# A four-layer gated cross-attention and FFN kernel: last residuals, LayerNorm roots and expert-weight loads put elsewhere in the engines' orders

## What is computed

```python
for l in range(4):
    x = x + tanh(g_xattn[l]) * xattn[l](layernorm(x), ctx, mask[l])   # 16 heads of 8
    x = x + tanh(g_ffn[l])   * ffn[l](layernorm(x))
# ffn[0]: silu(q4(x) q4(Wg)) * (q4(x) q4(Wu)), quantised by blocks of 16 again, times q4(Wd); 352 hidden
# ffn[1]: layernorm(x + relu(x W1 + b1) W2 + b2) * gamma + beta; 512 hidden
# ffn[2]: fp8(x * s) fp8(W) / (s * sw) + bias, s from the largest |x| of all batches
# ffn[3]: 16 experts of 128, the best 4 of a token, and 2 shared ones: silu(x Gate) * (x Up) Down
```

## Time and profile before

| what | value |
|---|---|
| median of 3 runs | 836.82 us |
| lowest and highest of them | 831.85 and 840.69 us |
| the profiled execution, whole | 837.56 us |
| its span (first to last instruction) | 835.8 us |
| PE, DVE, ACT, POOL busy, share of the span | 77%, 68%, 38%, 28% |
| mean granted clock of PE, 1 is full speed | 0.833 |

### The profile page before, as it was taken

One profiled execution on the slowest core, in us unless ns is written; L12 is line 12 of the kernel. 1 busy time (PEld: TensorE's weight loads), 2 busy tenths in 40 slices (PEclk: granted clock), 3 DMA queues, 4 the chain that ended last, 5 costly groups with the idle time before them and its releaser, 6 DMA issues. The chain is left out here.

```text
span 835.8 us, 9972 instructions
## 1 busy us (share of the span) xinstructions
PE 644.8 (77%) x2926; PEld 401.8 (48%) x2926; DVE 564.6 (68%) x1521; ACT 321.0 (38%) x611; POOL 236.1 (28%) x438
## 2 busy tenths in 40 slices
PE   5778786466769999784888880358887898989997
PEld 3434333244655664453544430124334576767875
DVE  8674788988772563486736645873557798878655
ACT  3043362133224425363144340213545455545554
POOL 4301233111111223104250631001122444545463
PEclk9576796878869999896599995555998889999999
DMA  8864321002203332005135320121500133343341
GB/s 252 177 186 129 57 71 30 0 1 64 63 12 100 109 58 82 13 1 161 28 105 151 76 78 0 50 77 58 167 14 3 53 105 98 93 124 104 113 120 57
DMA packets 67989, 67.71 MB, mean 81 GB/s; under 512 B 25119, under 2 KB 48223, under 8 KB 67552
## 3 DMA queue, kind: packets, MB, share of 16 engines
q1 hardware_dynamic: 61326, 64.61, 27.9%
q10 hardware_dynamic: 6610, 2.47, 1.2%
HBM read 50.29 MB, written 17.60 MB: 81 GB/s over the span
## 5 line engine op out<-in xcount | busy, mean ns | idle before, releaser
L1167 DVE TENSOR_REDUCE mraw<-ps 128x4 f32<-128x308 f32 x256 | 115.7, 475 | 81.6 <-PE ps L1550 33.0
L734 ACT ACTIVATE PT<-ps 110x512 f32<-110x512 f32 x192 | 110.9, 596 | 142.6 <-PE ps L1590 69.1
L1550 PE MATMUL ps<-KG,QG 98*128 98x308 f32 x256 | 115.3, 491 | 50.4 <-DVE mraw L1167 36.3
L1550 PEld LDWEIGHTS ps<-KG,QG 98*128 98x128 f32 x256 | 61.3, 246 | 95.9 <-DVE mraw L1167 72.6
L644 POOL TENSOR_TENSOR sg<-sg,cb 128x512 f32<-128x512 f32 x64 | 83.3, 1304 | 78.2 <-ACT sg L892 75.1
L1590 PE MATMUL ps<-QG,KG 128*110 128x512 f32 x192 | 95.6, 519 | 6.6 <-ACT PT L734 5.1
L1406 DVE TENSOR_TENSOR ps<-ps,sg 128x512 f32<-128x512 f32 x72 | 50.2, 698 | 39.2 <-POOL sg L644 36.0
L1610 PE MATMUL ps<-PT,VN 128*18 128x512 f32 x512 | 73.3, 647 | 0.0
L508 POOL CAST mhl<-mraw 128x64 fp32r<-128x64 f32 x16 | 5.0, 314 | 223.1 <-DVE mraw L1167 210.4
L1590 PEld LDWEIGHTS ps<-QG,KG 128*110 128x110 f32 x192 | 36.1, 192 | 51.9 <-ACT PT L734 37.1
L892 ACT ACTIVATE sg<-ps 128x512 f32<-128x512 f32 x72 | 43.2, 599 | 46.1 <-PE ps L1809 45.3
(11 more groups left out here) (277 smaller groups left out, 1411.9 us busy)
## 6 DMA issues: line engine op xcount, KB each, us to landing
cb<-c_parts SPq DMA_DIRECT2D x64, 256.0 KB, 3.3
QG<-q_parts SPq DMA_DIRECT2D x48, 256.0 KB, 3.9
KG<-k_parts SPq DMA_DIRECT2D x48, 154.0 KB, 3.0
q_parts<-hiT SPq DMA_DIRECT2D x14, 256.0 KB, 2.0
q_parts<-loT SPq DMA_DIRECT2D x14, 256.0 KB, 2.0
k_parts<-kmH SPq DMA_DIRECT2D x16, 154.0 KB, 2.3
k_parts<-kmL SPq DMA_DIRECT2D x16, 154.0 KB, 2.6
VN<-v_parts SPq DMA_DIRECT2D x16, 144.0 KB, 2.7
```

Source lines behind the costliest of these rows:

```text
L734: act.activation(PT[0:w, q % PTR, :], ps[0:w, 4 + q % 2, :], ACT.Exp, scale=SCALE[l]).then_inc(exp_done, 1)
L1167: dve.tensor_reduce(mraw[:, n % 2, i, g * HG:(g + 1) * HG], ps[:, u % 2, 0:GK].rearrange("p (h k) -> p h k", k=K), AX_X, ALU.max).then_inc ...
L1550: ins = pe.matmul(o, QG[0:KS, n % 3, g, q], KG[0:KS, n % 3, g, :], start=True, stop=l not in (1, 2))
```

## The change

1. The fourth residual of FFN0, FFN1 and FFN2 leaves the end of the FFN. DVE does it in slot 0 of the next layer, after step 3 and behind `q_rest(2)`; POOL refines and shifts its root in slot 0 after the split of the maxima, and ACT normalises at step 8 of slot 0. PE's wait for the PSUM banks moves from the start of slot 0 to the two groups of weighted sums that write them (layer 2 keeps its wait).
2. Nine batches' roots go from DVE to POOL: (2, 0) to (2, 3), (4, 1), (5, 1) and (7, 1) to (7, 3). DVE's list shrinks from 1121 instructions to 1022, POOL's grows from 437 to 565.
3. The gate weights' load goes from ahead of layer 2 to slot -1, behind the copies of batch 0's maxima; the up weights' load and split go from slot 1 to slot 2.

```diff
-        OWN = [(0, 0), (0, 1), (4, 0), (5, 0), (4, 1), (5, 1)] + [(2, b) for b in range(B)] + [(7, b) for b in range(B)]
+        OWN = [(0, 0), (0, 1), (4, 0), (5, 0), (7, 0)]
...
             for l in range(L):
-                if l == 2:
-                    sp.wait_ge(f1_ps, B)
-                    sp.dma_start(mst[:, :, :], a["moe_gate"]).then_inc(ld_moe, 16)
-                    sp.dma_start(low[:, :, :], a["low"].partition_broadcast(P)).then_inc(ld_moe, 16)
                 for k in range(-2, B):
                     if k + 2 < B and l * B + k + 2 >= 2:
                         queries_in(l * B + k + 2)
@@ -443,7 +439,11 @@
                         maxima_in(sp, l * B + k + 1, range(G))
                     if l == 1 and k in (-1, 1):
                         next_mask(4 + (k + 1) // 2)
-                    if l == 2 and k == 1:
+                    if l == 2 and k == -1:
+                        sp.wait_ge(f1_ps, B)
+                        sp.dma_start(mst[:, :, :], a["moe_gate"]).then_inc(ld_moe, 16)
+                        sp.dma_start(low[:, :, :], a["low"].partition_broadcast(P)).then_inc(ld_moe, 16)
+                    if l == 2 and k == 2:
                         sp.wait_ge(moe_lo, 1)
                         sp.dma_start(mst[:, :, :], a["moe_up"]).then_inc(ld_moe, 16)
                     if k >= 0 and l * B + k + 3 < N:
...
                     if 0 <= k + 1 < B:
                         split_maxima(n + 1)
-                    if l == 2 and k == -1:
-                        refine((5, B - 1))
-                        shift((5, B - 1))
+                    if l >= 1 and k == 0:
+                        refine((2 * l + (l > 1), B - 1))
+                        shift((2 * l + (l > 1), B - 1))
...
                     if l == 2 and k == 0:
                         split_experts(gH, gL, 0)
-                    if l == 2 and k == 1:
+                    if l == 2 and k == 2:
                         split_experts(uH, uL, 1)
                     if k >= 1:
                         refine((2 * l + (l > 1) + 1, k - 1))
@@ -627,6 +627,9 @@
                         pool.wait_ge(hq_scaled, j + 1)
                         pool.tensor_tensor(h, v, hscale[:, j % 2, :].unsqueeze(2).to_broadcast([P, 44, 16]),
                                            ALU.mult).then_inc(hq_done, 1)
+                        if j in (3, 5, 7):
+                            refine((2, j // 2 - 1))
+                            shift((2, j // 2 - 1))
                 if l == 1:
                     for m in LN_ORDER[4 * B:6 * B]:
                         if m not in OWN and m != (5, B - 1):
@@ -635,6 +638,9 @@
                 if l == 2:
                     pool.wait_ge(am_part, 1)
                     pool.partition_all_reduce(am[:, 2:3], am[:, 0:1], P, RMAX).then_inc(am_all, 1)
+                    for b in (1, 2):
+                        refine((7, b))
+                        shift((7, b))
...
-                        if c == 8 and k == -1 and l >= 1:
+                        if c == 8 and k == 0 and l >= 1:
                             normalise_out((2 * l + (l > 1), 3))
...
+            def residual0(b):
+                xs = x[:, b * TPB:(b + 1) * TPB, :]
+                dve.wait_ge(f0_ps, b + 1)
+                dve.scalar_tensor_tensor(out=xs, in0=ps[:, 6 + b % 2, :].rearrange("p (t d) -> p t d", d=D),
+                                         scalar=tg[:, 4:5], in1=xs, op0=ALU.mult, op1=ALU.add).then_inc(f0_done, 1)
+                dve.wait_ge(f0_done, b + 1)
+                next_input(1, b)
...
+            def residual1(b):
...
+                next_input(3, b)
+                if (5, b) in OWN:
+                    refine_own((5, b))
+
+            def residual2(b):
...
+                next_input(5, b)
+                if (7, b) in OWN:
+                    refine_own((7, b))
...
                 def after(k, c):
+                    if c == 3 and k == 0 and l >= 1:
+                        (residual0, residual1, residual2)[l - 1](B - 1)
...
                 for u in range(2 * TPB):
                     maximum(0, u // G, u % G)
-                residual(2)
+                residual0(2)
                 for u in range(2 * TPB, 4 * TPB):
                     maximum(0, u // G, u % G)
-                residual(3)
...
                 for u in range(4 * TPB):
                     maximum(0, u // G, u % G)
-                residual(3)
...
                 for u in range(4 * TPB):
                     maximum(0, u // G, u % G)
-                residual(3)
...
                     if n >= 1 and s == 0:
                         pe.wait_ge(o_out, 2 * n - 1 + f)
+                    if b == 0 and s == 0 and l == 1:
+                        pe.wait_ge(f0_done, B - 1 + f)
+                    if b == 0 and s == 0 and l == 3:
+                        pe.wait_ge(f2_read, B - 1 + f)
...
                 for k in range(-1, B + (l < 3)):
-                    if l == 1 and k == 0:
-                        pe.wait_ge(f0_done, B)
                     if l == 2 and k == 0:
                         pe.wait_ge(f1_read, B)
-                    if l == 3 and k == 0:
-                        pe.wait_ge(f2_read, B)
```

More of the change, by code:

```diff
@@ L1283, in rounded @@
                     dve.wait_ge(hq_scaled, j + 1)
[L1285 to L1292, removed]
                 for j in range(T // 2):
@@ L1300, in ffn0 @@
                     if j == 3:
-                        residual(0)
+                        residual0(0)
                     if j == 5:
                         q_rest(0)
-                        residual(1)
+                        residual0(1)
                 q_rest(1)
@@ L1323, in inner_sum @@
                         refine_own((4, b))
[L1325 to L1335, removed]
                 inner_sum(0)
-                residual(0)
+                residual1(0)
                 inner_sum(1)
@@ L1341, in ffn1 @@
                 q_rest(0)
-                residual(1)
+                residual1(1)
                 inner_sum(3)
-                residual(2)
+                residual1(2)
                 q_rest(1)
@@ L1354, in ffn2 @@
                 link(dve.tensor_tensor(am[:, 6:7], am[:, 0:1], am[:, 12:13], ALU.mult))
-                def residual(b):
-                    xs = x[:, b * TPB:(b + 1) * TPB, :]
-                    y = ps[:, 6 + b % 2, :].rearrange("p (t d) -> p t d", d=D)
-                    fb = rows[:, R_FB2, :].unsqueeze(1).to_broadcast([P, TPB, D])
-                    dve.wait_ge(f2_ps, b + 1)
-                    dve.scalar_tensor_tensor(out=y8[:, :, :], in0=y, scalar=am[:, 6:7], in1=fb, op0=ALU.mult, op1=ALU.add).then_inc(f2_read, 1)
-                    dve.wait_ge(f2_read, b + 1)
-                    link(dve.scalar_tensor_tensor(out=xs, in0=y8[:, :, :], scalar=tg[:, 6:7], in1=xs, op0=ALU.mult, op1=ALU.add))
-                    next_input(5, b)
-                    refine_own((7, b))
                 def quantised(b):
@@ L1375, in ffn2 @@
                 quantised(1)
-                residual(0)
+                residual2(0)
                 quantised(2)
-                residual(1)
+                residual2(1)
                 q_rest(0)
                 quantised(3)
-                residual(2)
+                residual2(2)
                 q_rest(1)
```

14 lines of the change are left out of this document (added).

## The result

The changed kernel took 845.52 us, the median of 4 runs (841.34 to 847.92), beside 834.34 for the kernel before (4 runs): 1.0123 of before, 95% interval 1.0083 to 1.0164. Timed again over 12 runs it took 842.97, 1.0104 of before (1.0070 to 1.0138). So it is slower by some 8 to 10 us, where 828, a gain of 9, was forecast, and outside the range of 820 to 836.

A forecast was written before the change was run, and what follows sets the result against it. No engine is full; time was taken as many short places where one engine holds the others. The terms summed to +9.0 us, from 837.56 to 828.6, about 828 on the median; range 820 to 836.

The forecast's parts named there:

- The stall in slot 0: Slot 0, layers 1 to 3: ACT normalises late, holding exponentials and PE; -7.0 us in all, from 0 to 10 lost.
- PE has a second bank for turned scores: Slot 0: this bank, one exponential ahead, cuts lateness of 2.4, 3.8 and 2.6 us to PE losses of 1.8, 3.2 and 2.0.
- FFN0: Roots of batches 0 and 1 on POOL: DVE loses 4.1 us of work, ACT gets results 3.9 later; taken as 0.
- The contention rival: Moved roots all run beside DVE's two-input work; three slots lose 1.0 us more each, FFN0 3.9; 835 us, chance .13.
- The up weights: Middle of layer 2: DVE stands about 10 us for the root of (6,1) in slot 3; -5.2 us, loss 4.2 to 10.
- the gate load: Boundary of layers 1 and 2: query parts no longer wait behind this load on SP; +5.1 us, 2 to 7.6.
- the residuals' 3.52 and 1.33 us: PE's waits at the FFN0 and FFN1 boundaries, 242.54 and 410.85, go when the fourth residual leaves there.
- the bare instruction of POOL: Boundary 2 to 3: its 7.03 us before line 509 moves to idle time behind the all-reduce; +7.0 us, 2 to 7.
- The rival that it is charged behind its neighbour's wait: Behind the all-reduce: POOL's reload delays the root of (7,1), leaving 2 of the 7 us; 833 us, chance .08.
- The slower case: Layer 2, slots 2 and 3: up weights land late, PE stalls beyond some 14 us; at 25, 848 us; chance .06.

The follow-up runs named there:

- late_norm: Changed kernel with ACT's normalising of batch 3 at step 11 of slot 0 instead of step 8: 834.70 us, 0.9969 of before.
- resid_only: Kernel before with only the three fourth residuals moved to slot 0, all nine roots on DVE, normalised at step 8: 843.82 us, 1.0097 of before.
- resid_late: Kernel before with only the three fourth residuals moved to slot 0, all nine roots on DVE, normalised at step 11: 831.03 us, 0.9973 of before.
- up_first: Changed kernel with POOL's root of (6,1) ahead of the up weights' split in slot 2 of layer 2: 832.57 us, 0.9959 of before.
- own_ffn0: Changed kernel with the roots of (2,0) and (2,1) refined by DVE again: 839.53 us, 1.0064 of before.
- up_only: Kernel before with only the up weights' load and split moved from slot 1 to slot 2: 843.69 us, 1.0099 of before.
- gate_only: Kernel before with only the gate weights' load moved to slot -1 of layer 2: 830.31 us, 0.9939 of before.
- after_again: The changed kernel as it is, timed again: 842.97 us, 1.0104 of before.
- own_ffn1: Changed kernel with the roots of (4,1) and (5,1) refined by DVE again: 837.12 us, 1.0016 of before.

## Why the prediction was wrong

The direction was wrong, mainly by two steps; a third added 3 us.

**The stall in slot 0 was priced too low: 5.2 us in layers 2 and 3 together, for 19.** The mechanism was named (ACT at step 8, exponentials of steps 9 to 11 behind, PE behind them), and the lateness was short by 0.9 and 1.9: 3.8 and 2.6 forecast, 4.7 and 4.5 measured (in layer 3 step 8 came 4.6 us behind the remainder, not the 6.7 of before: PE's granted clock was 0.90 from 576 to 582, and before it was 0.58 from 580 to 585). The step that failed is "PE has a second bank for turned scores, one exponential of 0.54 to 0.60 us ahead, so PE loses 1.8, 3.2 and 2.0": the bank hid nothing that shows, and PE did the work behind the wait at 1.2 GHz. That makes 6.9 us in layer 2 and 12.5 in layer 3. late_norm and the pair of resid_only and resid_late show that the stall is the cause; of the 12.5, about 5 hang on how long the low clock lasted, since up_first lost 7.9 behind the same wait. The prediction priced the clock nowhere. In layer 1 the sum was near, 1.8 for 1.3, though by the wrong reading: it compared with the start of the exponential of 262.34 where the two others took the end, and ACT's wait for the shift, forecast for all three layers, is not there.

**FFN0 was put at 0 and cost 4 to 6 us.** The bounds were -3.9 to +4.1. I took the free root, 4.0 us, and for contention the mean over the 63 instructions of line 565 on the page, 0.25 for 0.20. Here DVE's products run beside it, and the root took 6.5 us, so ACT gets each shift 4.4 us later and not 2. I also left POOL's own multiply behind the root out of account. own_ffn0's trace shows the size, its median 3 us. The contention rival named this mechanism, at 3.9 us, and was wrong on the three slots: there the roots took 4.0 us.

**The up weights, 5.2 for 8.3.** Load time, wait of DVE (about 10, measured 9.99) and its place were right. I stayed near the lower end, with nothing but PE's other work as a reason; up_only's trace loses the same 8.2 us in slot 3, so nearly all of the wait counts. That the split itself slows DVE's normalising in this slot (2.9 us of the 8.3, up_first) was in no term.

**Right:** the gate load (5.1, with gate_only alone 5 us of time), the residuals' 3.52 and 1.33 us, and the bare instruction of POOL. Of POOL's 7 us I had overlooked that the residual of FFN2 lay beside them; both went in the same change, so the sum still came out, by luck. The rival that it is charged behind its neighbour's wait is refuted by the root of (7,1) at 540.70. The Trainium skill, GPSIMD Engine Reference, section 2.1 Instruction dispatch, gives the load of about 6 us; the trace agrees in size and shows in addition that it runs in idle time ahead of a wait, while the rival put it behind the wait, an order that the page does not state.
The rule of the Trainium skill, SBUF — State Buffer, section SBUF: two separate sides, on the port pair that GpSimd and DVE share, is borne out by the POOL rows from 184.71 on, 0.20 free and up to 0.95 beside DVE's products of two SBUF tiles; by it FFN0 should have been priced at the contended end.

**The slower case** was priced as one mechanism in layer 2. The slower result came from three ordinary places together. The range was built from one case at a time, as if two losses could not come together. Even together the worst bounds of slot 0 (10), FFN0 (3.9) and the up weights (10) give about 840 and not the 843 to 845 measured, as the stall's own price lay outside its bound.

## What to carry to other kernels

When an instruction moves to another slot, read what the in-order engine that consumes it has queued behind: three steps later for ACT's normalising was worth 10 to 13 us. Price a new wait of the matrix engine with what follows it at the lower clock, not only by its length: waits of 4.4 to 4.5 us cost 6.9, 7.9 and 12.5 us here. And put a short chain that others wait for ahead of a long copy on the same queue (5.4 us in up_first), then look at what the other engine does while POOL copies: one DVE instruction of 0.34 us took 5.27.

## What had not been expected of the hardware

A wait of PE of 4.50 us was followed in layer 3 by a granted clock of 0.54 from 587 to 592 and 0.50 from 592 to 607, but the like wait of 4.52 us in layer 2 by 5 us at 0.50 only, with 1.00 in slot 1:

```profile
427.00:432.00 5.00, 2.81 (x10) 0.51 (x10) 0.00 (x0) 3.68 (x8) 4.91 (x2) 0.50 0.29 90
...
436.00:450.00 14.00, 12.05 (x70) 6.83 (x63) 7.11 (x16) 5.42 (x10) 0.64 (x2) 1.00 0.23 75
```

In up_first the spell is short in layer 3 too, behind a wait of 4.41 us; after_again, own_ffn0 and own_ffn1 have the long one. Why one spell lasts and the other doesn't, no run here settles.
